# The expert outputs gathered inside the next attention instead of in a stage of their own

## What is computed

```python
x = x + L0_xattn(ln(x), ctx)          # linear attention on sparsified queries and keys
x = x + L0_ffn(ln(x))                 # routed: top 2 of 8 experts, silu(g) * u, capacity C
x = x + L1_xattn(ln(x), ctx, mask)    # softmax(tanh(q.k) * exp(log_C)), 16 heads of 16
x = x + L1_ffn(ln(x))                 # shared experts with LoRA
x = x + L2_xattn(ln(x), ctx)          # softmax, 16 heads of 64, gated
x = x + L2_ffn(ln(x))                 # routed: top 2 of 8, gelu
x = x + L3_xattn(ln(x), ctx, mask)    # softmax, 16 heads of 16, mask, biases
x = x + L3_ffn(ln(x))                 # ternary weights, depthwise convolution
...
# L0_ffn, once the experts have written yb: each row adds its two outputs
ys = yb[jnp.minimum(slot, E * C - 1)] * (weights * kept)[:, None]
out = jnp.zeros((T, D), x.dtype).at[tokens].add(ys)
...
# L2_ffn: h is its input, cw the two weights
out = sum_e (gelu(h @ w1[e].T + b1[e]) @ w2[e].T + b2[e]) * cw[e] + h
return layernorm(out, ln_w, ln_b)     # eps 1e-12
```

## Time and profile before

| | us |
|---|---|
| median of 3 runs | 2900.87 (2896.5 to 2906.04) |
| the profiled execution | 2931.14, its span 2929.4, mean granted clock 0.935 |
| L0: attention | 0 to 310.7 |
| L0: route, experts, combine | to 425.7, 832.9, 901.8 |
| L1: tanh attention, shared experts | to 1112.6, 1273.6 |
| L2: attention | to 1904.7 |
| L2: route, experts, combine | to 2022.8, 2296.4, 2391.6 |
| L3: attention, ternary feed-forward | to 2756.8, 2929.4 |

### The profile page before, as it was taken

One profiled execution on the slowest core, in us unless ns is written; L12 is line 12 of the kernel. 1 busy time (PEld: TensorE's weight loads), 2 busy tenths in 40 slices (PEclk: granted clock), 3 DMA queues, 4 the chain that ended last, 5 costly groups with the idle time before them and its releaser, 6 DMA issues. The chain is left out here.

```text
span 2929.4 us, 47164 instructions
## 1 busy us (share of the span) xinstructions
PE 2512.4 (86%) x15874; PEld 1754.4 (60%) x15874; DVE 1372.3 (47%) x4867; ACT 1130.7 (39%) x2617; POOL 797.8 (27%) x867
## 2 busy tenths in 40 slices
PE   6999749999956998979999999883999559999786
PEld 4676428888832554647666565562999336666544
DVE  6988512222232654546643333442111367777665
ACT  4555211111105991234443434331333126666431
POOL 3443140000041210027754444404000401221242
PEclk8999879999977998989999999996999779999898
DMA  4222352222023210043310000044888310000000
GB/s 138 82 101 102 133 197 108 93 84 94 24 85 118 67 54 1 1 134 133 113 36 6 11 6 6 1 155 172 322 325 325 127 35 11 8 11 6 1 7 19
DMA packets 69939, 252.57 MB, mean 86 GB/s; under 512 B 16395, under 2 KB 32040, under 8 KB 52264
## 3 DMA queue, kind: packets, MB, share of 16 engines
q1 hardware_dynamic: 60008, 226.24, 22.2%
q0 software_dynamic: 9744, 23.87, 2.6%
HBM read 197.97 MB, written 52.10 MB: 85 GB/s over the span
## 5 line engine op out<-in xcount | busy, mean ns | idle before, releaser
L2732 PE MATMUL L_ffne_up<-L_ffne_xT,L_ffne_wu 128*128 128x128 f32 (+1 forms) x2144 | 389.8, 337 | 7.3 <-DMA L_ffne_wu<-in_L_ffn_up 7.3
L2732 PEld LDWEIGHTS L_ffne_up<-L_ffne_xT,L_ffne_wu 128*128 128x128 f32 x2144 | 328.1, 193 | 54.3 <-DMA L_ffne_wu<-in_L_ffn_up 6.9
L1082 POOL TENSOR_SCALAR L_xattn_p<-L_xattn_p,L_xattn_rec 112x375 f32<-112x375 f32 x256 | 311.8, 1225 | 0.0
L1387 PEld LDWEIGHTS L_xattn_pt<-ident,L_xattn_p 112*125 112x125 f32 x1536 | 197.3, 189 | 166.4 <-ACT L_xattn_p L1165 75.7
L2717 PE MATMUL L_ffne_dn<-L_ffne_wd,L_ffne_hT 128*112 128x256 f32 (+1 forms) x1200 | 266.3, 379 | 1.5 <-issue 1.5
L1387 PE MATMUL L_xattn_pt<-ident,L_xattn_p 112*125 112x112 f32 x1536 | 247.3, 289 | 20.5 <-DVE L_xattn_pt L1241 16.0
L1224 DVE TENSOR_REDUCE L_xattn_least<-L_xattn_s 112x1 f32<-112x375 f32 x256 | 128.4, 543 | 284.7 <-PE L_xattn_s L1375 284.4
L2717 PEld LDWEIGHTS L_ffne_dn<-L_ffne_wd,L_ffne_hT 128*112 128x112 f32 (+1 forms) x1200 | 216.8, 183 | 39.7 <-issue 2.1
L1241 DVE COPY L_xattn_pt<-L_xattn_pt 125x336 f32<-125x336 f32 x448 | 210.6, 497 | 52.6 <-PE L_xattn_pt L1387 52.4
L1165 ACT ACTIVATE L_xattn_p<-L_xattn_s,L_xattn_least 112x375 f32<-112x375 f32 x256 | 145.1, 570 | 186.2 <-DVE L_xattn_least L1224 186.1
L2620 POOL DMA_DIRECT2D L_ffn_ybuf<-L_ffne_y x75 | 40.1, 534 | 641.3 <-DVE L_ffne_y L2670 386.8
(11 more groups left out here) (369 smaller groups left out, 4480.0 us busy)
## 6 DMA issues: line engine op xcount, KB each, us to landing
L_ffne_wd<-in_L_ffn_down SPq DMA_DIRECT2D x43, 1024.0 KB, 4.9
L_ffne_wu<-in_L_ffn_up SPq DMA_DIRECT2D x35, 1024.0 KB, 5.2
L_ffne_wu<-in_L_ffn_up SPq DMA_DIRECT2D x8, 2048.0 KB, 7.9
L_xattn_kt<-L_xattn_kd SPq DMA_DIRECT2D x8, 1500.0 KB, 7.9
L_xattn_v<-L_xattn_vd SPq DMA_DIRECT2D x8, 1500.0 KB
L_ffn_xbuf<-L_ffnr_zeros SPq DMA_DIRECT2D x8, 1120.0 KB, 12.7
fa_ctxT<-in_ctxT SPq DMA_DIRECT2D x16, 375.0 KB, 3.6
fa_rows<-in_ctx_rows SPq DMA_DIRECT2D x16, 375.0 KB
```

What stands on the lines that cost most here:

```text
L1082: p = pool.tensor_scalar(p_sb[:, head % RP, :], p_sb[:, head % RP, :], rec[:, h, head:head + 1], None, ALU.mult)
L1387: m = pe.transpose(pt_ps[head % 2][0:KP, 0, kt * S:(kt + 1) * S], p_sb[:, head % RP, kt * KP:(kt + 1) * KP], ident[0:S, 0:S])
L2732: m = pe.matmul(up_ps[s % RING][k][:, 0, 0:RH], wu[:, h, c, k * FF + f * 128:k * FF + (f + 1) * 128], xT[:, h, c, q * RH:(q + 1) * RH], st ...
```

## The change

- Both `combine` stages go, with a barrier each.
- `tanh_attention`: GpSimd gathers for batches 0 to 3 before everything else, and two batches more in each of the bodies 0 to 5. DVE adds (`add_experts`) batches 0 to 3 before the first norm, and then two at the end of each of the bodies 0 to 5. The square root is taken in three groups: batches 0 to 3 at the start, 4 to 7 and 8 to 15 in the middle of bodies 2 and 6. The loop on GpSimd and ACT is written out.
- The L3 attention: ring of 3. Six batches are asked for first, one more in each body 0 to 9. DVE adds batches 0 and 1, norms them (`add_normed`) and adds 2 and 3 before the bodies; the rest goes between the heads (`beside`): `add_experts` in bodies 0 to 10, one `add_normed` for nearly each batch. The square roots, two kinds, come in pairs of batches on ACT at head 8 of bodies 0, 2, ... 12. The scores with the mask go straight into `p` (6 slots, no `ssb`). `ln_w` is one operand of a fused instruction, so the norm and its addition to x are two instructions and not four; `ln_b` is added to x already in L2's `route`, 16 additions between the slots and `tw.prepare`.
- The parts: L0's `route` takes the 14 parts of batch 7 (56 in all), L2's takes the 24 of `KeysValues` (64). `AHEAD` is 4 parts in both. The ternary weights' sum stands before part 12 of `BEHIND`.
- Wide keys and values get three slots, kept from the L0 attention to the end of L0's experts; a batch's values are stored in three transfers; only `run_experts`, at its end, waits for the stores. `r.xf` of L0 is freed with `route`.

The tanh attention:

```diff
+        RING, OPENING = 4, 4
+        GROUP = (0, OPENING, 2 * OPENING, NB)
+        got = sb("got", [S, RING, 2, D])
+        half = sb("half", [S, 2, D])
+        got_in, summed, stats_done = core.got_in["L0_ffn"], sem("summed"), sem("stats")
+        def arriving(b):
+            return range(OPENING + 2 * b, min(OPENING + 2 * b + 2, NB))
...
+                def gather(b):
+                    after(pool, summed, b - RING + 1)
+                    for k in range(2):
+                        pool.indirect_dma_start(
+                            out=got[:, b % RING, k, :], out_offset=None, in_=r.ybuf,
+                            in_offset=bass.IndirectOffsetOnAxis(r.get[:, k, b:b + 1], 0)).then_inc(got_in[b % RING], 16)
+                for b in range(OPENING):
+                    gather(b)
...
+                def deviations(n):
+                    act.wait_ge(stats_done, n + 1)
+                    span = slice(GROUP[n], GROUP[n + 1])
+                    act.activation(core.std[:, span], mv[:, span, 1], ACT.Sqrt,
+                                   bias=core.eps[0:S, :]).then_inc(std_done, 1)
+                deviations(0)
...
+                        if c == 2 and b in (2, 6):
+                            deviations(1 if b == 2 else 2)
+                for b in range(NB):
+                    body(b, b % 2)
...
+                def add_experts(b):
+                    h = b % 2
+                    dve.wait_ge(got_in[b % RING], 32 * (b // RING + 1))
+                    ch.link(dve.scalar_tensor_tensor(out=half[:, h, :], in0=got[:, b % RING, 0, :], scalar=r.p[:, 0, b:b + 1],
+                                                     in1=x[:, b, :], op0=ALU.mult, op1=ALU.add))
+                    dve.scalar_tensor_tensor(out=x[:, b, :], in0=got[:, b % RING, 1, :], scalar=r.p[:, 1, b:b + 1],
+                                             in1=half[:, h, :], op0=ALU.mult, op1=ALU.add).then_inc(summed, 1)
+                    dve.wait_ge(summed, b + 1)
+                    ch.link(dve.bn_stats(core.st46[:, h, :], x[:, b, :]))
+                    ch.link(dve.bn_aggr(mv[:, b, :], core.st46[:, h, :]))
+                    if b + 1 in GROUP:
+                        dve.sem_inc(stats_done, 1)
+                def invert(n):
+                    dve.wait_ge(std_done, n + 1)
+                    span = slice(GROUP[n], GROUP[n + 1])
+                    dve.reciprocal(rstd[:, span], core.std[:, span]).then_inc(rstd_done, 1)
+                    dve.wait_ge(rstd_done, n + 1)
                 def normalize(b, h):
+                    if b in GROUP:
+                        invert(GROUP.index(b))
...
+                    for later in arriving(b):
+                        add_experts(later)
+                for b in range(OPENING):
+                    add_experts(b)
                 normalize(0, 0)
```

The last attention; its `gather` is the same with `RING` 3, and `add_experts` writes `r.xf`:

```diff
+            got, ln_w = sb("got", [S, RING, 2, D]), sb("ln_w", [S, D])
+            tiny, std3, rstd3 = sb("tiny", [S, 1]), sb("std3", [S, NB]), sb("rstd3", [S, NB])
+            got_in = core.got_in["L2_ffn"][0:RING]
+            ln_in, tiny_done, summed, var_done, root_done, stats_done = (
+                sem(n) for n in ("ln_in", "tiny", "summed", "var", "root", "stats"))
...
+        OPENING = 6
...
+                    if OPENING + b < NB:
+                        gather(OPENING + b)
...
+                    act.wait_ge(tiny_done, 1)
+                    root_of_sums(0)
+                    root(0)
...
+                        if not wide and head == 8 and b % 2 == 0 and b + 2 < NB:
+                            root(b // 2 + 1)
+                            if b + 4 < NB:
+                                root_of_sums(b // 2 + 2)
...
+                if not wide:
+                    root_of_sums(1)
...
+                    y0, y1, to = got[:, b % RING, 0, :], got[:, b % RING, 1, :], r.xf[:, b, :]
+                    dve.wait_ge(got_in[b % RING], 32 * (b // RING + 1))
+                    ch.link(dve.scalar_tensor_tensor(out=y0, in0=y0, scalar=r.p[:, 0, b:b + 1], in1=to,
+                                                     op0=ALU.mult, op1=ALU.add))
+                    dve.scalar_tensor_tensor(out=to, in0=y1, scalar=r.p[:, 1, b:b + 1], in1=y0,
+                                             op0=ALU.mult, op1=ALU.add).then_inc(summed, 1)
+                    dve.wait_ge(summed, b + 1)
+                    ch.link(dve.bn_stats(core.st46[:, b % 2, :], to))
+                    ch.link(dve.bn_aggr(core.mv2[:, b, :], core.st46[:, b % 2, :]))
+                    if b % 2:
+                        dve.sem_inc(var_done, 1)
+                def add_normed(b):
+                    n, to = b // 2, r.xf[:, b, :]
+                    if b == 0:
+                        dve.wait_ge(ln_in, 16)
+                    if b % 2 == 0:
+                        dve.wait_ge(root_done, n + 1)
+                        ch.link(dve.reciprocal(rstd3[:, b:b + 2], std3[:, b:b + 2]))
+                    ch.link(dve.scalar_tensor_tensor(out=to, in0=to, scalar=core.mv2[:, b, 0:1], in1=ln_w[:, :],
+                                                     op0=ALU.subtract, op1=ALU.mult))
+                    ch.link(dve.scalar_tensor_tensor(out=x[:, b, :], in0=to, scalar=rstd3[:, b:b + 1], in1=x[:, b, :],
+                                                     op0=ALU.mult, op1=ALU.add))
+                    ch.link(dve.bn_stats(core.st46[:, 2 + b % 2, :], x[:, b, :]))
+                    ch.link(dve.bn_aggr(core.mv[:, b, :], core.st46[:, 2 + b % 2, :]))
+                    if b % 2:
+                        dve.sem_inc(stats_done, 1)
+                def beside(b, pair):
+                    if pair == 0 and b == 0:
+                        add_experts(4)
+                    if pair == 2 and 5 + b < NB:
+                        add_experts(5 + b)
+                    if b == 0 and pair in (4, 6):
+                        add_normed(pair // 2)
+                    if b % 2 == 0 and pair == 14 and b + 4 < NB:
+                        add_normed(b + 4)
+                    if b % 2 == 1 and pair == 6 and b + 4 < NB:
+                        add_normed(b + 4)
...
+                    if not wide and b % 2 == 0:
+                        dve.wait_ge(std_done, b // 2 + 1)
+                        ch.link(dve.reciprocal(core.rstd[:, b:b + 2], core.std[:, b:b + 2]))
...
+                        after(dve, t_out, b * H + head - PP + 1)
                         dve.memset(core.tick[:, head:head + 1], 0.0)
-                        dve.tensor_tensor_reduce(out=ssb[:, head % 4, :], in0=s, in1=hide[:, h, :], scale=1.0,
+                        dve.tensor_tensor_reduce(out=at_p(b, head), in0=s, in1=hide[:, h, :], scale=1.0,
...
+                if not wide:
+                    for b in range(2):
+                        add_experts(b)
+                    for b in range(2):
+                        add_normed(b)
                 normalize(0, 0)
                 normalize(1, 1)
+                if not wide:
+                    for b in range(2, 4):
+                        add_experts(b)
```

Keys and values, routing, experts:

```diff
-        self.spans = {"r_": (0, 10), "c_": (10, NB)}
+        self.spans = {"r_": (0, NB)}
...
+        self.ks = core.sb(ctx, pre + "ks", [128, self.SLOTS, self.IC, SK])
+        self.vs = core.sb(ctx, pre + "vs", [KP, self.SLOTS, KT, self.INNER])
+        self.k_stored, self.v_stored = core.spilled["k"], core.spilled["v"]
...
     def store_values(self, sp, b):
-        sp.wait_ge(self.done, (b - self.first + 1) * len(self.parts))
-        sp.dma_start(self.vd[b], self.vs[:, b % 2, :, :]).then_inc(self.v_stored[b % 2], 16)
+        for kt in range(KT):
+            sp.wait_ge(self.done, (b - self.first) * len(self.parts) + self.IC + 2 * kt + 2)
+            sp.dma_start(self.vd[b, :, kt, :], self.vs[:, b % self.SLOTS, kt, :]).then_inc(self.v_stored[b % self.SLOTS], 16)
...
-            turns = len([b for b in range(self.first, self.end) if b % 2 == i])
+        for i in range(self.SLOTS):
+            turns = len([b for b in range(self.count) if b % self.SLOTS == i])
             after(sp, self.k_stored[i], turns * 16)
-            after(sp, self.v_stored[i], turns * 16)
+            after(sp, self.v_stored[i], turns * 16 * KT)
...
-        BESIDE, AHEAD = parts[0:NB], parts[NB:NB + 8]
-        BEHIND = parts[NB + 8:]
+        BESIDE, AHEAD = parts[0:NB], parts[NB:NB + 4]
+        BEHIND = parts[NB + 4:]
...
+                if not twice:
+                    for b in range(NB):
+                        c.step(dve.tensor_tensor(x[:, b, :], x[:, b, :], after_b[:, :], ALU.add))
...
-                    if tw and n == len(BEHIND) - 4:
+                    if tw and n == 12:
                         tw.sum(pe, lg_ps[0])
...
+                if spilled:
+                    spilled.wait_stored(sp)
```

What goes with `combine`, and the order of the stages:

```diff
-            @block.gpsimd
-            def _(pool):
-                for b in range(NB):
-                    after(pool, summed, b - RING + 1)
-                    for k in range(2):
```

(50 more changed lines are left out.)

196 lines of the change are left out of this document (72 added, 124 removed).

## The result

The changed kernel takes 2866.77 us (median of 4 runs, 2861.66 to 2871.49) against 2902.11 (4 runs, 2896.50 to 2906.04) of the kernel before on the same chip. The ratio is 0.988, 95% interval 0.985 to 0.991: 35 us less, where 77 less were forecast. The profiled execution took 2863.27, span 2861.3, clock 0.945.

What follows compares the result with a forecast made beforehand. Combine stages bound first by GpSimd's queue, tanh attention by ACT. Terms -164.1 + 15.7 - 5 + 1 + 0.5 - 1 + 41 = -111.9; 34.5 less in timed runs, -77.4 from 2900.87: forecast 2824, range 2783 to 2866.

Steps and rivals of the forecast that it cites:

- Stages that go: Both combine stages vanish: -164.1 us against the profiled execution, 34.5 of it not gained in the timed runs.
- the stops belong to the profiled execution: Engine stops in the combine stages, 34.5 us together, were taken as absent from the timed runs.
- Rival 1: Stops real in every run, so parts moved beside both scatters meet them, +15 and +25: 2833 us, chance 0.22.
- First routing and its experts: L0's route 5 us shorter through an earlier scatter, its experts +1 for weight loads behind batch 7's stores.
- Tanh attention: Later opening +8.9, added sums in the bodies +1, two later square roots with table loads +5.8: +15.7 us.
- Last attention: L3 attention: opening +9, vector blocks between the heads +22, square roots and table loads +10: +41 us.
- Half: Last attention: half of the 44.2 us of added DVE blocks would show, +22, with 8 and 40 as ends.
- Second routing: L2's route +0.5 us, with the ternary weights' sum later and 64 parts; its experts -1.
- 4: Gathers inside the attentions' loops bring the stops along, at 5 us a batch +110: 2934 us, chance 0.03.
- 5: Each activation table switch costs a drain of 1.38 us more, for 18 loads: 2849 us, chance 0.02.
- 2: The last attention hides the added work, 9 + 5 in place of 41: 2797 us, chance 0.12.
- 3: Every added block in the last attention is on the path, +36 with the tanh attention's 2: 2860 us, chance 0.11.

Runs made afterwards that it cites:

- e0: The kernel before, unchanged, profiled again on the chip with stops: 2929.08 us, timed runs' median 2935.99.
- e10: The kernel before, unchanged, profiled on a chip that times it at 2901.23 us: 2899.95 us.
- e3: The changed kernel with the two sums of a tanh attention body in two places, behind the transposed rows' copy and behind the division: 2884.07 us, ratio 0.982.
- e4: The changed kernel, unedited, on another chip: 2870.42 us against 2901.19 of the kernel before, ratio 0.990.
- e7: The changed kernel with the square roots inside the last attention's bodies replaced by plain copies: 2872.01 us.
- e8: The changed kernel with each sum and norm in the last attention's bodies cut in halves behind pairs 0, 2, 4, 6: 2872.96 us.
- e11: The changed kernel with one sum and one norm in every body of the last attention: 2862.77 us, ratio 0.986.
- e13: Changed kernel; stores of batches 6 and 7 deferred to the experts, tanh sums split, last attention's first sums before the bias, one sum and norm a body: 2820.38 us.
- e1: The changed kernel with batch 7's stores issued in the experts stage behind its first loads, on the chip with stops: 2887.72 us, ratio 0.984.
- e9: Changed kernel; batch 7's stores deferred to the experts, tanh sums split, last attention's first sums before the bias, its blocks in halves: 2837.94 us, ratio 0.978.
- e2: The changed kernel with each batch's values stored in one transfer, not three, on the chip with stops: 2901.35 us, one run.
- e12: The changed kernel without the vector work of the last attention's sums 4 to 15 and norms 2 to 15: 2831.77 us.

## Why the prediction was wrong

The direction held, and so did the two large terms; the size didn't. By the table the forecast misses 40 us of 77. In its own order:

- **Stages that go.** Right: -133.4 measured on chips without stops, -129.7 by the forecast's estimate. The step "the stops belong to the profiled execution" named the wrong owner, the chip (e0, e10), and came within 4 us of the number for the chips that timed the result by luck. Rival 1, "real in every run", is right for the chip of e0 to e3 (routings longer by 21 and by 17 to 20 us with the parts in them, +15 and +25 by the rival) and wrong for those of the result, e4 to e7, e8 to e10 and e11 to e13. What makes the engines stop beside indirect transfers on that chip stays open; nothing I ran tells it.
- **First routing and its experts, forecast -4, measured +20.** This is the step that failed, 24 us of the 40. I priced "1 us for batch 7's stores" by SyncE's issue times and "the experts' first weight loads stand behind those stores, +1". They share the queues with the scatter and the loads. Ahead of the barrier the scatter's last transfer took 9.6 us to land and not 2.5, which used up the 5.9 us that the scatter had gained. Behind it the first rows reached PE 18.5 us late. The cost was hidden from me because the wait for the stores, `wait_stored`, moved from the end of routing to the end of the experts. Deferring batch 7's stores removes the late rows (e1, e9, e13). The late landing goes only when batch 6's stores are deferred too (e13: routing 107.9; e9: 116.7, as in e8). Why batch 6's stores, which the kernel before has beside its scatter too, delay it now isn't shown. e2 speaks against the cut in three, on the chip with stops.
- **Tanh attention, forecast +15.7, measured +24.4.** Opening: +10.5 and not +8.9. The first rows land 4.6 us later into the stage than in the earlier trace rows; weight loads that weren't there run beside them, which no run took away. The bodies: +13.9 and not +6.8. I compared VectorE's free 6 us with 3.4 of work. A body is 11.5 us and not 13.2, and VectorE busy for 7.1 of it, so 4.4 us are free, which is still enough. The place was wrong: behind the division the work delays the next norm, for which PE and then ACT wait, 1.82 us at a time. e3's place takes 6 to 9 us back. The two bodies with a square root, forecast at 5.8 for both roots, take 3.2 and 3.4 more than 11.5 with the sums apart (e13), sums included, and 3.8 and 5.1 more in the change.
- **Last attention, forecast +41, measured +47.5.** The parts were further off than the sum, so that the sum came near is luck. The first norm came at +22.4 where +18.9 was forecast (11.6 us later than before, not 8.1). The first residual came 13.2 us later than in e10 (69.2 - 56.0) even without the blocks of the bodies. Square roots: 10 forecast, nothing without the blocks (e12), at most 0.8 a body beside them (e7). Blocks: 22 forecast for 26, and by e12 33.9 (411.0 - 377.1; 30.0 with e4's 407.1), 0.77 of their 44.2. Of this, 8.6 lie ahead of the first residual (77.8 - 69.2), where seven blocks stand and the clock fell once more. The other 25.3 fall in the bodies behind it, with 19 blocks. Three of these bodies took 26.1 to 26.5 us with a fall of the clock to 0.5 for 6.8 us, where the same body took 24.57 without, 5.0 us in sum; no term of mine held that. The remaining 20.3 are 0.63 of the blocks' 32.3, unevenly: 0.8 for the one block of an even body, 3.5 for the three of an odd one. "Half" is what they cost when they are spread evenly and the clock holds, 46.26 - 42.6 = 3.6 us for four blocks of 6.8 (e11).
- **Second routing, forecast +0.5 and -1:** 118.3 against 118.3, 273.3 against 272.1. Right within 2 us; in the changed kernels on chips without stops the routing is 118.3 to 121.5.
- **Rivals.** 4, gathers bringing stops into the loops: on the chip with stops (e1, e2, e3) the last attention took 408.1 to 415.2, elsewhere 407.1 and 411.0, the tanh attention with its sums together 240.6 and 240.5 (e1, e2), elsewhere 234.8 to 240.4. No issue of a gather in the changed kernel's attentions took over 1.34 us. It fell. 5 fell with e7. 2 and 3 are bounds that the last attention stayed between (14 and 75).

The range ended at 2866, the time was 2867. Its upper end was made of the last attention's bounds and held nothing for the step that failed. Those bounds were added up wrong besides: 9, 40 and 22 are 71, not 63.

## What to carry to other kernels

When a wait for transfers is moved past a barrier, the transfers still have to be done, beside whatever comes next. Price them by bytes and by how long such a transfer takes beside the same work, and put stores that nobody reads soon behind the loads that the next stage starts with. Work added to an engine with free time costs by its place in that engine's order: put it where the next instruction has no one waiting, and spread it evenly. Look at which stretch an instruction really falls in before naming what makes that stretch long. Take the profile that the sum is made against from the same chip as the times, above all when the two don't agree.

## What the runs showed of the hardware

- On one of the chips ScalarE and TensorE stop for 6 to 10 us at a time while indirect transfers run beside other transfers (e0 to e3); in the profiles of e4 to e13, on three others, they never did. The same kernel takes 2936 us there and 2901 here. Each chip was used in one session only.
- An issue of a transfer on SyncE takes 0.34 to 0.62 us at the start of the experts stage of the kernel before. Behind 3 MB of stores beside the scatter single issues took 6.58, 4.47 and 5.33, and a transfer of the scatter took 9.6 us to land and not 2.5.
- A two-operand vector instruction of 256 columns took 0.48 us alone and 1.17 and 1.04 at 2315.93 and 2317.14 of the changed kernel, while GpSimd multiplied the queries (2315.89, 2.00 us in place of 1.82 for the pair).
- TensorE's granted clock falls from 2.4 to 1.2 GHz in the middle of a stage that keeps it busy 84% of the time (346.54 of 411.00 us), behind a wait of 2.45 us (2383.00), and a pair of bodies with such a fall took 1.5 to 1.9 us more. Two waits of 2.35 us in the same stage (ahead of 2480.08 and 2575.46) had no fall behind them.
